# One attention stage of a fused kernel: TensorE's value and sum products in two rounds of its order, and VectorE's copy of the turned output one round later

## The reference

```python
B, S, D, H = 16, 128, 128, 16          # HD = D // H = 8
x = _layernorm(x)                      # for each of the 16 batches
q, k, v = split_heads(x @ Wq), split_heads(x @ Wk), split_heads(x @ Wv)
scores = einsum('bhqd,bhkd->bhqk', q, k) / sqrt(HD)
attn_w = softmax(scores, axis=-1)
ctx = einsum('bhqk,bhkd->bhqd', attn_w, v)
attn_out = ctx.reshape(b, s, d) @ Wo + bo
out1 = _layernorm(x + attn_out, ln1_g, ln1_b)
...                                    # then the router and the experts on out1
```

## Time and profile before

| what | value |
|---|---|
| median of 3 runs | 1611.06 us (1610.51 to 1611.57) |
| the profiled execution, own time | 1613.62 us |
| its span, first to last instruction | 1611.8 us |
| mean granted clock of TensorE over the span | 0.916 |
| first VALUES of this stage starts at | 1149.27 us |
| last VALUES of this stage starts at | 1329.98 us |

### The profile page before, as it was taken

How to read it: one execution, slowest core, us unless ns; L and a number is a source line. 1 busy time by engine, 2 the same in 40 slices (tenths; PEclk the granted TensorE clock), 3 DMA queues, 4 the chain that set the end, 5 groups by cost and what they waited for, 6 DMA issues and landing times. The chain is left out here.

```text
span 1611.8 us, 27953 instructions
## 1 busy us (share of the span) xinstructions
PE 1362.8 (85%) x9813; PEld 1081.0 (67%) x9813; DVE 834.6 (52%) x2211; ACT 722.9 (45%) x1641; POOL 119.9 (7%) x258
## 2 busy tenths in 40 slices
PE   6765799999996799699999988973777775999995
PEld 5641477777784487489999978862566663667664
DVE  4549677677663454545555443448566652122224
ACT  4331677777762312255555542431444441333433
POOL 1010000000001000000000002022222111000000
PEclk9879799999997999799999988975899986999998
DMA  8000000000000000000000005020000000000000
GB/s 325 1 1 0 1 2 1 1 1 1 2 1 1 1 1 0 1 1 1 1 1 2 1 1 119 1 102 3 1 1 2 1 2 0 1 1 1 1 0 27
DMA packets 6441, 24.73 MB, mean 15 GB/s; under 512 B 797, under 2 KB 1311, under 8 KB 5418
## 3 DMA queue, kind: packets, MB, share of 16 engines
q1 hardware_dynamic: 6314, 23.03, 4.2%
HBM read 21.98 MB, written 1.05 MB: 14 GB/s over the span
## 5 line engine op out<-in xcount | busy, mean ns | idle before, releaser
L1306 DVE SCALAR_TENSOR_TENSOR XN<-bank,gate,XN 128x128 f32<-128x128 f32 x256 | 89.8, 351 | 224.7 <-PE bank L1270 222.2
L1286 ACT ACTIVATE e_hidden<-bank,small 128x512 f32<-128x512 f32 x152 | 104.4, 687 | 214.5 <-PE bank L1258 214.5
L766 PE MATMUL bank<-a_va,a_pT 128*128 128x65 f32 x1024 | 130.3, 271 | 0.7 <-ACT a_pT L933 0.6
L1011 DVE TENSOR_REDUCE a_mx<-bank 128x4 f32<-128x512 f32 x128 | 87.9, 686 | 80.1 <-PE bank L806 80.1
L1270 PEld LDWEIGHTS bank<-attention_weights,e_hidden 128*128 128x128 f32 x1024 | 119.2, 192 | 14.8 <-issue 14.8
L766 PEld LDWEIGHTS bank<-a_va,a_pT 128*128 128x128 f32 x1024 | 125.2, 193 | 2.5 <-ACT a_pT L933 1.1
L1258 PE MATMUL bank<-XNT,attention_weights 128*128 128x512 f32 x256 | 121.2, 606 | 1.2 <-PEq L541 1.2
L1270 PE MATMUL bank<-attention_weights,e_hidden 128*128 128x128 f32 x1024 | 119.3, 275 | 0.0
L831 PE MATMUL bank<-attention_weights,a_cv 128*128 128x256 f32 x256 | 84.4, 411 | 15.0 <-issue 15.0
L933 ACT ACTIVATE a_pT<-bank 128x512 f32<-128x512 f32 x128 | 76.2, 595 | 41.9 <-PE bank L840 39.2
L1019 DVE TENSOR_TENSOR a_shifted<-bank,a_mx 128x512 f32<-128x512 f32 x128 | 88.3, 690 | 3.4
(11 more groups left out here) (353 smaller groups left out, 2610.9 us busy)
## 6 DMA issues: line engine op xcount, KB each, us to landing
attention_weights<-in_a SPq DMA_DIRECT2D x2, 2048.0 KB, 10.9
mod_ring<-in_mod_weights SPq DMA_DIRECT2D x4, 576.0 KB
ctx_both<-in_ctx SPq DMA_DIRECT2D x1, 2048.0 KB, 9.7
attention_weights<-in_up SPq DMA_DIRECT2D x1, 2048.0 KB, 8.1
attention_weights<-in_down SPq DMA_DIRECT2D x1, 2048.0 KB, 13.4
down<-in_down SPq DMA_DIRECT2D x1, 1536.0 KB, 17.2
down<-in_mod_weights SPq DMA_DIRECT2D x2, 576.0 KB
X<-in_x SPq DMA_DIRECT2D x4, 256.0 KB, 3.8
```

What stands on the lines that cost most here:

```text
L766: last = pe.matmul(value_bank[:, j * (W + 1):(j + 1) * (W + 1)], pT[:, i.slot(2), j * 128:(j + 1) * 128], va[:, p, g // 2 * 8 + 2 * j + g ...
L1011: dve.tensor_reduce(mx[:, i.slot(2), :], score_bank[i.slot(2)][:, :].rearrange("p (h s) -> p h s", h=4), AX.X, ALU.max).then_inc(maxed, 1)
L1286: act.activation(hidden[0:rows, p, f, :], up_bank_of(i, f)[0:rows, :], function, bias=up_bias(g, f)).then_inc(hidden_ready, 1)
L1306: dve.scalar_tensor_tensor(out=total, in0=down_bank[j][:, e * D:(e + 1) * D], scalar=gate_column(k, 4 * q + j, g * per_group + e), in1=tot ...
```

## The change

Two lags change and one is new. SUMS is a step of its own on PE with lag 7: the 16 matmuls with `ones` leave VALUES (round 1) and stand at the head of round 2, behind the TURN_P of round 1. KEEP gets lag 16 in place of 15: DVE takes the turned output at the end of round 3, behind that round's NORM_O, maximum and subtraction, and no longer at the end of round 2. TURN_OUT stays where it was. No instruction of any engine is added or removed.

```diff
-    PROJECT, KEEP_QKV, BLOCKS, SCORE, EXP, TURN_P, KEEP_P, VALUES, NORM_O, OUT, ADD, NORMALISE, AFFINE, KEEP, TURN_OUT = \
-        0, 1, 2, 3, 5, 5, 6, 6, 8, 8, 9, 10, 11, 15, 15
+    PROJECT, KEEP_QKV, BLOCKS, SCORE, EXP, TURN_P, KEEP_P, VALUES, SUMS, NORM_O, OUT, ADD, NORMALISE, AFFINE, TURN_OUT, KEEP = \
+        0, 1, 2, 3, 5, 5, 6, 6, 7, 8, 8, 9, 10, 11, 15, 16
...
+            def weigh(at_column, stationary, per_group, p):
+                for j in range(4):
+                    for c in range(4):
+                        first = c * per_group + 32 * j
+                        last = pe.matmul(value_bank[32 * c:32 * c + 32, at_column:at_column + S],
+                                         stationary[:, first:first + 32], pT[:, p, c, j * 128:(j + 1) * 128],
+                                         start=j == 0, stop=j == 3, tile_position=(0, 32 * c))
+                        if at_column and j == 3:
+                            last.then_inc(weighted, 1)
...
-                    for at_column, stationary, per_group in ((0, va[:, n % 3, :], 160), (S, ones[:, :], 0)):
-                        for j in range(4):
-                            for c in range(4):
-                                first = c * per_group + 32 * j
-                                last = pe.matmul(value_bank[32 * c:32 * c + 32, at_column:at_column + S],
-                                                 stationary[:, first:first + 32], pT[:, p, c, j * 128:(j + 1) * 128],
-                                                 start=j == 0, stop=j == 3, tile_position=(0, 32 * c))
-                                if at_column and j == 3:
-                                    last.then_inc(weighted, 1)
+                    weigh(0, va[:, n % 3, :], 160, p)
+                i = at(SUMS)
+                if i.alive and i.offset % 4 == 3:
+                    weigh(S, ones[:, :], 0, batch_of(i).slot(2))
                 i = at(TURN_P)
...
-            sweep(pe, G, 8, TURN_OUT, body, rolled=False)
+            sweep(pe, G, 8, KEEP, body, rolled=False)
```

More of the change, by code:

```diff
@@ L1872, in body @@
                     pool.tensor_copy(col(k.out1, n), out[:, p, :]).then_inc(copied, 1)
-            sweep(pool, G, 8, TURN_OUT, body, rolled=False)
+            sweep(pool, G, 8, KEEP, body, rolled=False)
         @block.tensor
@@ L1993, in body @@
                     act.activation(pT[:, q, g, :], turn_bank[p][:, :], ACT.Copy).then_inc(p_kept, 1)
-            sweep(act, G, 8, TURN_OUT, body, rolled=False)
+            sweep(act, G, 8, KEEP, body, rolled=False)
         @block.vector
@@ L2048, in body @@
                     dve.bn_aggr(stats[:, 6:8], stats[:, 0:6]).then_inc(spread, 1)
-            sweep(dve, G, 8, TURN_OUT, body, rolled=False)
+            sweep(dve, G, 8, KEEP, body, rolled=False)
 def choose_two(nc, k):
```

## The result

The changed kernel takes 1599.53 us (median of 4 runs, 1598.51 to 1600.55), against 1611.32 in the runs of the kernel before beside it: a ratio of 0.9927, with a 95% interval of 0.9909 to 0.9944. It is faster by 11.8 us. The forecast was 5.7 us, and its range ended at 1600.0, half a microsecond above the measured time. The profiled execution has a span of 1596.7 us and a mean granted clock of 0.926, against 0.916 before.

What follows compares the result with a forecast made beforehand. No engine is full; a closed chain of two legs, 5.34 and 5.87 us, plus slow-clock periods sets the pace. First leg +1.0, KEEP +2.5, clock -9.7, held back +0.5: -5.7, so 1605.4 us; range 1600 to 1614.

Steps and rivals of the forecast that it cites:

- The mechanism: PE ahead of VALUES: PROJECT's wait for KEEP splits 2.54 us idle into 1.2 and 1.3, removing slow periods, -9.7 us.
- The six slow periods named: VALUES to VALUES: six of eight periods with TensorE at 1.2 GHz become fast, 1.61 us each, 9.7 us to gain.
- PROJECT's delay: Second leg on PE: PROJECT starts 1.48 us later behind KEEP, covered by 0.6 and 0.5 us, so costing nothing.
- rival 2: Half of the slow stretches stay, three of six, giving -1.3 us: 1609.8, no change; chance 0.15.
- rival 3: All slow stretches stay and KEEP is paid on DVE in the second leg: +3.5 us, 1614.6; chance 0.12.
- rival 4: Covers of 0.5 and 0.6 us too thin; PROJECT's delay reaches VALUES by 0.3 us, +3.6, 1609; chance 0.05.
- The first leg: VALUES to SCORE, mostly PE: 5.41 us against 5.34 with SUMS moved, +1.0 us over fourteen periods.
- The gap g: On PE, between a full-width turned item and the 32-column SUMS: taken as 0.20 us, bounds 0 and 0.20.
- Half a microsecond held back: Clock term: 0.5 us taken back for one chance in three that one of six slow periods stays.
- KEEP and NORM_O lie in a hole of DVE and cost nothing: DVE before the change: both steps fit while the next maximum waits 1.06 us for SCORE, so they cost nothing.
- the 1.7 that the forecast allowed either way: Start of the stage behind: its slow stretch may shift, worth up to 1.7 us, half of 3.4, either way.
- Rival 1: First leg on PE: switches to 32 columns free, third item follows TURN_OUT at once; -10.7 us, 1600.4; chance 0.14.

Runs made afterwards that it cites:

- the run with the later wait: Changed kernel with KEEP ahead of SCORE's maximum, and PROJECT waiting from the fourth batch on for round 0's subtraction: 1629.48 us, ratio 1.0103.

## Why the prediction was half right

**The mechanism was right, and the experiments carry it.** The gain comes from neither leg's work but from PE's idle time. The six slow periods named are the six that went, and the two that were said to stay, the second and third of the fourteen, stayed. PROJECT waits for line 2044, KEEP's new line, for 1.28 us (forecast 1.2), and the other piece is 1.22 (1.3). KEEP costs 0.19 to 0.20 on DVE (0.21). PROJECT's delay is covered, and the run with the later wait found the cover where it was put. Rivals 2, 3 and 4 did not come about. The rule of the Trainium skill that stood beside rivals 2 and 3 (TensorE: Matmul & The Clock Gate, the second failure mode) is not borne out for two pieces of 1.2 us. With 0.36 and 1.95 us the clock did still swing, in five periods of fourteen.

**What failed is the sum: three terms were mis-sized, all in the same direction.**

1. *The first leg, +1.0 us, measured -2.0.* The forecast leg was 5.41 us and the measured one is 5.20 to 5.21. The gap g is there as booked: 1240.12 to 1241.21 is 1.09, and eight loads take 0.89, so 0.20 is left. This is what the page TensorEngine Tiling (Array Packing) of the Trainium skill, Key Properties, would have: a change of the tiling mode drains TensorE. But two other parts were too large. SUMS' loads take 0.81 and not 0.90; before, they came right behind those of `va`, and why they are shorter now is not shown. And the third item follows TURN_OUT's load after 0.11, not 0.23: the real transpose costs nothing at its border, and I had taken the middle of two bounds where the lower one held. Together 0.21 us, fourteen times: 3.0 us. The run with the sums alone has the same leg of 5.20.
2. *Half a microsecond held back* for a slow period that might stay. None did.
3. *The end of the stage, booked at nothing.* The prediction costed the fourteen periods and stopped there. From the fifteenth VALUES to the last KEEP the changed kernel saves another 1.7 us. In the last two batches there is no SCORE in whose shadow KEEP could wait, so the step "KEEP and NORM_O lie in a hole of DVE and cost nothing" is wrong for them. The pair of runs with KEEP in round 2 and in the hole differs by 1.3 us there. Another 1.0 us goes with a slow stretch of 3.4 us where there were 6.8: from the fifteenth to the sixteenth VALUES it is 9.63 us here, and 10.62 in the run with KEEP in the hole. Against them stand 0.5 us that the moved sums alone lose there (11.37 + 8.62 against 10.99 + 8.45 before); why they do is not known. And the next stage's slow start is 1.35 us shorter, which is inside the 1.7 that the forecast allowed either way but left out of the sum.

3.0 + 0.5 + 1.7 + 1.35 is 6.6, and the traces' -12.3 differs from the forecast -5.7 by that. The median lies 0.5 us below the range. Rival 1, at 1600.4, comes nearest in time, but half for another reason: the third item did follow TURN_OUT at once, as it said, while the switches to 32 columns were not free. That it came so near is chance.

**Parts of the change by themselves.** In medians, of about 1611.6: KEEP late with its wait -8.1, the sums alone -3.3. Together they are -11.4, and the whole change has -11.8.

## What to carry to other kernels

Look at how long TensorE is idle in one piece in each period of a loop, even where other engines set the pace. If the granted clock swings, a wait that delays some matmul by a microsecond, where it has cover, can be worth more than work taken away: here 9.6 us, against 3.3 for moving the sums. Test it by adding a wait or useless matmuls alone, and try more than one place: 0.7 us earlier the wait left five slow periods, and past its cover it made the kernel slower. Then follow the sum to the stage's end: in the last rounds some steps are missing, and what was hidden behind them is on the path.

## What the runs showed of the hardware

- The idle time ahead of VALUES and the slow periods among fourteen: 2.54 us, eight (before) or seven (the sums alone, and KEEP in the hole); 0.36 and 1.95 us, five; 1.65 us in one piece, none; 1.09 and 1.22 us, none. With 2.41 and 0.71 us nearly every period is slow, from the projections on. In two runs 3.2 us of idle time ahead of the fifteenth VALUES had no slow stretch behind it (a clock of 1.00 over 8.08 us), in another it had a clock of 0.75.
- Between full-width matmuls and those of 32 columns in float32 there are 0.20 us in both directions at 2.4 GHz. A transpose between two full-width groups has no such gap: 0.11 us to the next load, the pitch of all loads there.
